# A two-stage linear layer in a fast product scheme: small products in another order, sums built one product ahead, x sums on VectorE, fewer weight differences

## What is computed

```python
# x: (32, 128, 2048)
base  = einsum('bsi,oi->bso', x, W0) + bias                  # W0: (2048, 2048)
low   = einsum('bsi,bri->bsr', x, lora_a[itok_B_1_7])        # rank 16
delta = einsum('bsr,bor->bso', low, lora_b[itok_B_1_7])
x = x + base + scale[itok_B_1_7][:, None, None] * delta
x = x + einsum('bij,bkj->bik', x, W1[itok_B_1_14])           # W1: (16, 2048, 2048)
```

## Time and profile before

| what | value |
|---|---|
| median of 3 runs | 2782.98 us (2781.64 to 2783.62) |
| profiled execution | 2777.48 us, span 2775.7 us |
| mean granted TensorE clock | 0.972 of 2.4 GHz |
| VectorE busy in the span | 81% |
| ScalarE | 50% |
| GpSimd | 40% |
| HBM | read 650.42 MB, written 100.66 MB |

### The profile page before, as it was taken

How to read it: one execution, slowest core, us unless ns; L and a number is a source line. 1 busy time by engine, 2 the same in 40 slices (tenths; PEclk the granted TensorE clock), 3 DMA queues, 4 the chain that set the end, 5 groups by cost and what they waited for, 6 DMA issues and landing times.

```text
span 2775.7 us, 35408 instructions
## 1 busy us (share of the span) xinstructions
PE 2603.3 (94%) x12154; PEld 2132.6 (77%) x12154; DVE 2257.2 (81%) x1902; ACT 1392.5 (50%) x1486; POOL 1100.5 (40%) x718
## 2 busy tenths in 40 slices
PE   7886998899998989998999999999999999999999
PEld 5665787677877777776888888888878878878887
DVE  7877799998887899887878888777877877867865
ACT  3322333333433333335666666666666756756665
POOL 7647477764446687551032041130320311301402
PEclk9998999999999999999999999999999999999999
DMA  5786764354366544656877768768799999998996
GB/s 217 303 298 233 227 182 137 116 187 167 122 206 212 176 134 167 191 207 240 287 259 277 266 222 309 243 237 284 248 351 325 334 352 338 321 349 302 312 320 234
DMA packets 213715, 686.32 MB, mean 247 GB/s; under 512 B 23424, under 2 KB 31648, under 8 KB 213536
## 3 DMA queue, kind: packets, MB, share of 16 engines
q1 hardware_dynamic: 204032, 649.46, 65.4%
q0 software_dynamic: 9216, 33.56, 6.4%
q10 hardware_dynamic: 288, 1.05, 0.1%
HBM read 650.42 MB, written 100.66 MB: 271 GB/s over the span
## 4 chain that ended last, share of the span: by engine, by line
PE 66%; DVE 16%; DMA 7%; issue 6%; POOL 3%; SPq 1%; ACT 1%; DVEq 0%; POOLq 0%; ACTq 0%
PE acc L1195 16%; PE acc L1196 16%; PE acc L1197 16%; PE acc L1112 6%; PE acc L1114 6%; PE acc L1113 6%; DVE tx L1067 5%; DVE ws L1067 5%; DVE xb L987 3%; DMA wb<-w 2%; DVE acc L1057 2%; DMA xb<-x_sums 2%; DMA xb<-x 1%; PE acc L1151 1%; DMA acc<-w 1%
## 5 line engine op out<-in xcount | busy, mean ns | idle before, releaser
L1067 DVE TENSOR_TENSOR ws<-wb,ws 128x1024 fp32r<-128x1024 f32 x964 | 1312.0, 1389 | 300.8 <-ACT ws L923 288.0
L923 ACT CAST ws<-wb 128x1024 fp32r<-128x1024 f32 x964 | 985.9, 1050 | 992.6 <-PE acc L1197 421.8
L1195 PE MATMUL acc<-ws,ops 128*128 128x512 f32 (+1 forms) x2048 | 804.2, 393 | 30.7 <-DVE lows L1017 17.8
L1196 PE MATMUL acc<-ws,ops 128*128 128x512 f32 (+1 forms) x2048 | 800.9, 391 | 0.0
L1197 PE MATMUL acc<-ws,ops 128*128 128x512 f32 (+1 forms) x2048 | 800.1, 391 | 0.0
L829 POOL TENSOR_TENSOR wb<-wb,eye_s 128x128 f32<-128x128 f32 x384 | 316.9, 855 | 1206.2 <-DMA wb<-w 1205.9
L1112 PE MATMUL acc<-tx,ws 128*128 128x512 f32 x1568 | 635.7, 405 | 132.7 <-DVE tx L1067 66.5
L1113 PE MATMUL acc<-tx,ws 128*128 128x512 f32 x1568 | 627.2, 400 | 0.0
L1114 PE MATMUL acc<-tx,ws 128*128 128x512 f32 x1568 | 627.0, 400 | 0.0
L1112 PEld LDWEIGHTS acc<-tx,ws 128*128 128x128 f32 x1568 | 305.6, 195 | 218.2 <-DVE tx L1067 80.5
L1195 PEld LDWEIGHTS acc<-ws,ops 128*128 128x128 f32 x2048 | 386.7, 189 | 112.1 <-DVE lows L1017 19.1
(11 more groups left out here) (64 smaller groups left out, 1249.4 us busy)
## 6 DMA issues: line engine op xcount, KB each, us to landing
wb<-w SPq DMA_DIRECT2D x816, 512.0 KB, 7.7
xb<-x SPq DMA_DIRECT2D x78, 512.0 KB, 5.5
wb<-w_sums SPq DMA_DIRECT2D x64, 512.0 KB, 7.0
xb<-x POOLq DMA_DIRECT2D x64, 512.0 KB, 8.7
y<-acc SPq DMA_DIRECT2D x32, 1024.0 KB, 8.1
out<-ost SPq DMA_DIRECT2D x128, 256.0 KB, 7.3
xst<-xt SPq DMA_DIRECT2D x60, 512.0 KB, 6.6
ystage<-y SPq DMA_DIRECT2D x60, 512.0 KB, 11.0
```

What stands on the lines that cost most here:

```text
L923: eng.copy(hi, src).then_inc(s_hi, 1)
L1067: eng.tensor_tensor(lo, src, hi, ALU.subtract).then_inc(s_lo, 1)
L1195: eng.matmul(dst, yh, wh, start=begin, stop=False)
L1196: eng.matmul(dst, yh, wl, start=False, stop=False)
```

## The change

- The seven small products come in another order, with another form of the scheme: the first two use loaded quarters alone (`T_SLOT`, `W_SLOT`), and the chain of sums is t3, t2, t4, t1 and s1, s2, s4, s3. `b21` and `a12` are used by small product 1.
- t3, t2 and s1 of a product are due in the last two small products of the one before; the rest in its own first three. All x sums are VectorE's, due 8 us into a small product. z and w are VectorE's too.
- `beside` makes s1, s2 and s3 on GpSimd wait until a named small product's last matmul is done; s4 has no such wait. The four evictions of a small product are due together behind its end.
- Only two weight differences are made (`d` = 0 and 1, 16 subtractions on VectorE, each from two loaded tiles, one stored). Products with n = 3, 4, 5 build their weights by a plain load and an accumulating DMA of GpSimd's ("wacc", 8 for each). Identities are added for n = 0, 2, 4, 6 only.
- The first low-rank blocks stand two small products earlier, at the end of stage 1.

```diff
-X_FREE = {"b11": 3, "b12": 4, "b22": 5, "b21": 6}
-W_FREE = {"a11": 3, "a21": 4, "a22": 5, "a12": 6}
-T_SLOT = ("b11", "b11", "b11", "b22", "b12", "b21", "b11")
-W_SLOT = ("a11", "a21", "a21", "a21", "a11", "a12", "a22")
+X_FREE = {"b22": 3, "b12": 4, "b11": 5, "b21": 6}
+W_FREE = {"a21": 3, "a22": 4, "a11": 5, "a12": 6}
+T_SLOT = ("b11", "b21", "b11", "b11", "b12", "b22", "b21")
+W_SLOT = ("a11", "a12", "a11", "a21", "a11", "a12", "a22")
...
-W_SUM = {2: 0, 3: 1, 4: 2, 5: 3}
-UNIT = (1, 0, -1, 2, 1, 2, 1)
+W_PLAIN = (("w", 0, 0), ("w", 0, 1), ("d", 0), ("d", 0), ("w", 0, 0), ("d", 0), ("w", 1, 1))
+W_ADDED = {3: ("w", 0, 0), 4: ("w", 1, 0), 5: ("d", 1)}
+UNIT = (1, 0, -1, 0, 1, 0, 1)
...
     def ev_key(s, ot):
-        return te[at["W", s, ot]] + 0.5
+        return te[at["W", s, 3]] + 0.4 + 0.1 * ot
+    def made_key(d, p):
+        return (18.0 + 9.0 * p, 32.0 + 15.0 * p)[d]
...
+        if n in W_ADDED:
+            for role in W_ROLE:
+                for h in range(2):
+                    adds.append((lo_key("W", s0 - K + W_FREE[role], h) + 9.0, "wacc", (q, role, h)))
         for h in range(2):
-            adds.append((lo_key("W", s0, h) + 1.3, "s3", (q, h)))
-            adds.append((lo_key("W", s0, h) + 4.0, "s1", (q, h)))
-            adds.append((lo_key("W", s0 + 1, h) + 1.3, "s2", (q, h)))
-            adds.append((lo_key("W", s0 + 2, h) + 1.3, "s4", (q, h)))
+            adds.append((past(s0 - 2 + h, 0.3) if q else -8.5 + 4.0 * h, "s1", (q, h)))
+            adds.append((past(s0 + h, 0.3) if q else lo_key("W", 0, h) + 8.0, "s2", (q, h)))
+            adds.append((past(s0 + 1 + h, 3.0 if h == 0 else 2.9), "s4", (q, h)))
+            adds.append((past(s0 + 2 + h, 0.3), "s3", (q, h)))
         for c in range(2):
-            sums1.append((lo_key("T", s0, c) + 2.0, "t1", (q, c)))
-            sums2.append((lo_key("T", s0 + 1, c) + 2.0, "t2", (q, c)))
-            adds.append((lo_key("T", s0 + 1, c) + 5.0, "t3", (q, c)))
-            adds.append((lo_key("T", s0 + 2, c) + 4.0, "t4", (q, c)))
+            sums.append((past(s0 - 2, 8.0 + 0.1 * c) if q else -12.0 + c, "t3", (q, c)))
+            sums.append((past(s0 - 1, 8.0 + 0.1 * c) if q else -9.0 + c, "t2", (q, c)))
+            sums.append((past(s0, 8.0 + 0.1 * c), "t4", (q, c)))
+            sums.append((past(s0 + 1, 8.0 + 0.1 * c), "t1", (q, c)))
...
+            def beside(eng, s):
+                if s >= 0:
+                    eng.wait_ge(s_mm, at["W", s, 3] + 1)
...
+                if kind == "wacc":
+                    q, role, h = index
+                    eng.wait_ge(s_wb[WS[q][role]][h], 16 * (q + 1))
+                    eng.dma_start(w_tile(q, role, h), w_source(eng, q, role, h, W_ADDED[q % K]),
+                                  accum_op=ALU.add).then_inc(s_wa[WS[q][role]][h], 16)
+                    continue
...
                 elif kind == "s2":
                     q, h = index
-                    eng.wait_ge(s_lo, number["W", K * q + 1, h] + 1)
-                    s1, a22, s3 = w_tile(q, "a21", h), w_tile(q, "a22", h), w_tile(q, "a11", h)
-                    ins = eng.tensor_tensor(s1, a22, s3, ALU.subtract)
+                    beside(eng, K * q - 1 + h)
+                    eng.wait_ge(s_lo, number["W", K * q, h] + 1)
+                    eng.wait_ge(s_pool, pool_no["s1", q, h])
+                    s1, a11 = w_tile(q, "a21", h), w_tile(q, "a11", h)
+                    ins = eng.tensor_tensor(a11, s1, a11, ALU.subtract)
```

More of the change, by code:

```diff
@@ L69, in slots_of @@
     return slots
-XS = [slots_of(("b11", "b12", "b22", "b21"), X_NEXT, q) for q in range(NG * K)]
+XS = [slots_of(("b11", "b12", "b21", "b22"), X_NEXT, q) for q in range(NG * K)]
 WS = [slots_of(("a11", "a12", "a21", "a22"), W_NEXT, q) for q in range(NG * K)]
@@ L208, in program @@
                 loads.append((key, "w", (q, role, h)))
[L209 to L214, removed]
+    for d in range(2):
+        for p in range(8):
+            for i in range(2):
+                loads.append((made_key(d, p) - 10.0 + 0.1 * i, "made", (d, p, i)))
+            loads.append((made_key(d, p) + 2.0, "keep", (d, p)))
     tile_no = [None] * NRAW
@@ L235, in program, with past @@
         raw_user[k], free_at[k] = what, key + 1.5
-    adds, sums1, sums2 = [], [], []
+    def past(s, after):
+        return max(t_of(s), -12.0) + after
+    adds, sums = [], []
     for q in range(NG * K):
@@ L264, in program @@
             for oh in range(2):
[L265 to L273, removed]
+                sums.append((t_of(K * (K * g + 3) + Z_AT[blk]) + 8.3 + 0.1 * oh, "z", (g, blk, oh)))
+                sums.append((t_of(K * (K * g + 4) + W_AT[blk]) + 8.3 + 0.1 * oh, "w", (g, blk, oh)))
+    for d in range(2):
+        for p in range(8):
+            sums.append((made_key(d, p), "made", (d, p)))
     for key, kind, index in splits:
@@ L279, in program @@
     for _, kind, index in adds:
-        if kind != "acc":
+        if kind not in ("acc", "wacc"):
             count += 1
             pool_no[(kind, *index)] = count
-    sums = sorted(sums1 + sums2)
+    sums.sort()
     sum_no = {(kind, *index): i + 1 for i, (_, kind, index) in enumerate(sums)}
-    made.sort()
-    made_no = {(kind, *index): i + 1 for i, (_, kind, index) in enumerate(made)}
     fast, slow = [], []
@@ L309, in program @@
             loads += [(la_key + kh, "la", (0, kh)) for kh in range(2)]
[L310 to L311 removed]
+            loads.append((la_key + 2.0, "xs", (0, 0)))
+            loads.append((la_key + 3.0, "xs", (0, 1)))
+            loads.append((t_of(K * (NG * K - 1) + 3) + 5.0, "y", (0, 0, 2)))
             loads.append((ev_key(NSTEP - 1, 0), "y", (0, 1, 0)))
@@ L543, in program @@
             vector_tasks.append((key, "ev", 0, (s, ot)))
-        for key, kind, index in sums + made:
+        for key, kind, index in sums:
             vector_tasks.append((key, kind, 0, index))
@@ L1002, in _ @@
+                if what == "made":
+                    d, p = index
+                    made_loaded(eng, d, p)
+                    one, other = made_tile(d, p, 0), made_tile(d, p, 1)
+                    eng.tensor_tensor(other, one, other, ALU.subtract).then_inc(s_sum, 1)
                     continue
```

278 lines of the change are left out of this document (127 added, 151 removed).

## The result

The changed kernel takes **2748.48 us** (median of four runs, 2743.67 to 2760.95) against 2782.31 for the kernel before (four runs): a ratio of 0.989, 95% interval 0.987 to 0.991. It is faster by 34 us. The forecast was 2747; it had the right sign, and its four terms come out as follows.

What follows compares the result with a forecast made beforehand. TensorE, 94% busy, was taken as the bound, with 199 us of stage 1 excess winnable. Gains 41 + 5 + 31 less loss 41 make 36 us: 2741.5, plus 5.5 for the median, 2747; range 2672 to 2805.

Steps and rivals of the forecast that it cites:

- Part 4: Products 3, 4, 10 and 11: eight accumulating weight loads each, 22 us on full DMA engines, cause late starts; loss 41 us.
- part 5: Products 0 to 2: 50 of 80.9 us excess left (18 start, 10 difference waits, 16 stall, 6 elsewhere); gain 31 us.
- Part 3: New order and sums made ahead: gain 41 us in products 5 to 9 and 12, gain 5 in product 13.
- The sign named for it: TensorE's waits gathered at small product 1 of products 3, 4, 10 and 11, DMA share near 1 for 70 us ahead.
- Loads fit: Rival: accumulating loads take little from plain transfers, so 59 + 12 us are not lost; 2676 us, chance 0.22.
- fourth case: Rival: GpSimd's queue starves the DMA engines, its accumulates standing behind sums that wait for weights; 2807 us, chance 0.20.
- Part 2: GpSimd's weight sums wait for a small product's end; 84 of 112 run beside evictions, costed at nothing for VectorE.
- part 1: VectorE's stage 1 work: 887 us if GpSimd is out of the way, fitting into 1065.
- third case: Rival: VectorE becomes the bound, all 112 GpSimd sums meeting two-input work, 1133 us; 2783 us, no change, chance 0.12.

## Why the prediction was right

**The sum.** The two large terms, a gain of 41 and a loss of 41, came with their sign and near their size. That the total came within 1.5 us is luck. Part 4 lost 7 us less than forecast, part 5 gained 4 less and product 13 gained 6 less, which leaves 2 of the 36. The 5.5 us added for the median were not there (the profiled execution took 2748.32 us), but stage 2 was 5.3 us longer in it.

**Part 3, the order and sums made ahead** (gain 41 in products 5 to 9 and 12; measured 41.6, 19.3 us left of 60.9). The sign that it named, 77 to 81 us a product, came: 394.5 / 5 = 78.9 (81.0 in the cut of the prediction, which holds product 10's late start). The run with the sums made later shows that about half of the gain of this stretch, 21.9 us, needs the lead, and the run without GpSimd's waits gives 14.6 of it back. No run tries the order of the small products or the evictions due together, so what the rest needs is not shown. The other sign, splits near 1.3 us, did not come: in products 5 to 9 they take 1.58 (weight) and 1.62 (x), and nothing is lost in 7 and 8 all the same.

**Part 4, accumulating loads on full engines** (loss 41; measured 34.2). The backlog was sized well. The last accumulating loads of products 3, 4, 10 and 11 land at 320.6, 408.8, 903.1 and 994.2 us; the starts without their stalls would be 294.0, 390.2, 877.9 and 973.9. That is +26.6, +18.6, +25.2 and +20.3, where +28.4 and +20.7 were forecast. The step that failed is the one that turned this into stalls: "the new one in small product 1, so loaded by about +7". The sign named for it did not come: the stalls stand ahead of small product 0, at `b11`, which is freed only at small product 5, so that its accumulating loads are the fifth and sixth of the eight of x and share the backlog. Having waited 8.5 to 10.7 us there, TensorE finds `b21` only 0.4 to 3.8 us late at small product 1. Together 45.9 us of waits for the 59 forecast; the extra busy time at a lower clock, 162.34 + 162.89 − 2 × 152.3 = 20.6 us in the four products, was put at 12. Plain second loads gave 30 of the four products' 76 us over back, sums built in an idle stretch all but 1 of the 39 of products 10 and 11, the saves taken out a part, and t3's wait and GpSimd's issue none: these runs show engine time in that window as the cause, with the chain's share in the rest open. "Loads fit" and the fourth case fall with it.

**Part 5, products 0 to 2** (gain 31, 50 left; measured 27.3, 53.4 left). Together they take 292.7 us in the cut of the prediction, under the 300 named. Inside, the 50 came otherwise than split. Product 0 starts at 11.98, product 1 at 113.66, product 2 at 211.16 us, and product 2's small product 6 at 282.96. So product 0 is 25.5 us over (18 were left at the start), product 1 with the wait ahead of product 2 is 21.3 over (10 and 16), and the rest of product 2 6.5 (6). The wait right ahead of product 2 is 6.2 us. No run tested these terms one by one.

**Part 2, GpSimd's sums at nothing.** Here the working failed and the forecast did not. VectorE is busy for 1032 us of stage 1, not the 887 of part 1: of the 84 s1, s2 and s3, 61 take over 2.6 us, where a sum beside evictions takes 2.4 and one among splits 3.4. The third case, with all 112 sums caught, put VectorE at 1133: it came six tenths of the way (145 of 246). In the changed kernel's product 8 the mechanism is seen as it was meant, s2 at 2.42 us beside four evictions:

```profile
730.04 2.47 DVE L1064 TENSOR_TENSOR acc<-acc 128x512 f32<-128x512 f32 x4
...
730.97 2.42 POOL L794 TENSOR_TENSOR wb<-wb 128x1024 f32<-128x1024 f32 x1 [8.47 <-PE acc L1122]
...
732.43 2.04 DVE L1075 TENSOR_TENSOR tx<-xb,tx 128x1024 fp32r<-128x1024 f32 x1
```

The split behind it still grows from 1.21 to 2.04 us: the sum ends at 733.39, after the split has begun, and the split ends 1.08 us behind it. The sum starts 0.93 us into the evictions and outlasts them by 0.88. The rule of the Trainium skill, "SBUF — State Buffer", section "Who interferes with whom", holds in these rows. Products 7 and 8 lose nothing by it, since VectorE has room there (60.46 us busy of product 7's 76.10); what the runs show of its price is the 18 us more without the waits.

**Part 3, product 13** (gain 5; measured a loss of 0.6). It was treated as late sums. Its one long wait, 5.9 us ahead of small product 1, ends with an x split: the last accumulated tiles of x land at 1161.6 and 1164.1 us, 11 and 13 us past the product's start. From 1110 to 1150 us the engines are full (a share of 1.05), with five 1 MB stores of outputs among the loads. Product 6, of the same kind (n = 6), waits 4.5 us at the same place, after a share of 1.02 from 515 us on. This is read from the trace; no run tried it.

## What to carry to other kernels

Before a sum is moved from compute engines into accumulating DMAs, add up the DMA engines' time in the window in which its tiles must arrive, at the accumulating price: idle engines a product later don't help, but the same transfer placed there does. Sums that stand between a wait and its user are best made one step of the pipeline ahead: taking that lead away cost 48.5 us here, taking away the waits that keep two engines apart 18. And a long wait in a profile is worth an experiment before it is believed: t3's 36.5 us and GpSimd's idle issue time were both worth nothing.
